# Three routing groups of 5, 5 and 6 batches instead of four of 4, and two elementwise steps of the experts exchanged between VectorE and GpSimd

## The reference

```python
h = layernorm(x) * (1 + ca) + sa
# attention: every token goes to 2 of 8 experts, by softmax of h @ gate
# per batch and expert: the last 256 of its tokens, in order of the sequence
q, k, v = q_w h, k_w[e] h, v_w[e] h          # q and k then squared into features
S = 0                                        # linear attention, chunk by chunk
out = (q k^T * causal) v + q S ; S = S + k^T v
x = x + ga * (rms_per_head(sum_2(weight * out)) @ o_w)
h = layernorm(x) * (1 + cb) + sb
h = swiglu(h @ lin0)
# experts: 8 routed ones, 4 chosen per token, and 2 shared ones
routed = sum_e combine[t, e] * ((silu(h w1_e) * (h w3_e)) @ w2_e)
h = swiglu((routed + shared) @ lin1)
x = x + gb * h
```

## Time and profile before

| | us |
|---|---|
| median of 3 runs | 1236.74 (1235.38 to 1238.14) |
| the profiled execution | 1226.49 |
| its span, first to last instruction | 1224.7 |
| busy: TensorE, VectorE, ScalarE, GpSimd | 1073.1, 913.7, 674.7, 489.9 |

### The profile page before, as it was taken

The page is one execution under the profiler, slowest core; times in us unless marked ns, Lnnn a source line. Parts: engine busy times, 40 slices in busy tenths (PEclk is TensorE's granted clock), DMA queues, the critical chain, the costliest instruction groups (busy, mean ns, idle before and its releaser), DMA issues. The chain is left out here.

```text
span 1224.7 us, 26738 instructions
## 1 busy us (share of the span) xinstructions
PE 1073.1 (88%) x9288; PEld 778.6 (64%) x9288; DVE 913.7 (75%) x2058; ACT 674.7 (55%) x1645; POOL 489.9 (40%) x450
## 2 busy tenths in 40 slices
PE   4865779999999877889999995988998899899997
PEld 3653546667777655667666664765666577677774
DVE  4785568788877666668778784888888987786774
ACT  2452245455555545656667552666666566555564
POOL 2046213312332444431221114656676644455552
PEclk9987679999999999999999997999999999899999
DMA  9972133323333333322222215321332322225230
GB/s 304 367 303 91 35 93 99 110 87 101 102 111 95 98 95 96 88 77 71 70 67 66 66 35 155 89 63 52 111 97 71 90 80 84 72 86 149 78 86 18
DMA packets 83586, 125.76 MB, mean 103 GB/s; under 512 B 9088, under 2 KB 65920, under 8 KB 79360
## 3 DMA queue, kind: packets, MB, share of 16 engines
q1 hardware_dynamic: 73216, 98.86, 26.5%
q0 software_dynamic: 10240, 25.18, 6.4%
HBM read 71.32 MB, written 52.69 MB: 101 GB/s over the span
## 5 line engine op out<-in xcount | busy, mean ns | idle before, releaser
L1489 DVE SCALAR_TENSOR_TENSOR att<-reach,endrel,wide 128x1024 f32<-128x1024 f32 x160 | 204.8, 1280 | 85.8 <-PE wide L1401 76.8
L1607 POOL TENSOR_TENSOR kvw<-kvw,hq 128x512 f32<-128x512 f32 x128 | 170.6, 1333 | 183.2 <-ACT kvw L1698 177.2
L900 POOL DMA_INDIRECT gst<-attended_rows,idxs x128 | 138.6, 1083 | 237.1 <-DVE att L1489 155.0
L252 POOL DMA_INDIRECT routed_rows<-hq,idxs x128 | 130.7, 1021 | 223.5 <-DVE att L1489 152.8
L1732 DVE TENSOR_TENSOR epp<-kvw,epp 128x512 fp32r<-128x512 f32 x160 | 138.2, 863 | 80.4 <-ACT epp L1706 77.8
L1654 PE MATMUL bank<-epp,w2p 128*128 128x512 f32 x480 | 166.3, 456 | 11.0 <-DVE epp L1732 10.9
L1644 PE MATMUL bank<-hp,w1p 128*128 128x512 f32 x480 | 142.0, 405 | 8.3 <-POOL hp L1560 6.2
L1376 PE MATMUL bank<-kvw,turned 128*128 x320 | 142.0, 526 | 5.1 <-ACT turned L1285 1.6
L1706 ACT ACTIVATE epp<-kvw 128x512 fp32r<-128x512 f32 x160 | 100.5, 628 | 79.1 <-DVE kvw L1739 74.4
L1644 PE MATMUL wide<-hp,w3p 128*128 128x512 f32 x480 | 141.4, 404 | 0.0
L1698 ACT ACTIVATE kvw<-bank 128x512 f32<-128x512 f32 x160 | 94.8, 593 | 79.8 <-PE wide L1644 79.3
(11 more groups left out here) (265 smaller groups left out, 1895.7 us busy)
## 6 DMA issues: line engine op xcount, KB each, us to landing
hq<-weight_rows SPq DMA_DIRECT2D x16, 2048.0 KB
routed_rows<-zero SPq DMA_DIRECT2D x4, 5120.0 KB, 24.6
rows<-routed_rows SPq DMA_DIRECT2D x80, 256.0 KB
attended_rows<-ob SPq DMA_DIRECT2D x80, 128.0 KB
out<-fin SPq DMA_DIRECT2D x16, 256.0 KB, 2.3
routed_rows<-hq,idxs POOLq DMA_INDIRECT x128
gst<-attended_rows,idxs POOLq DMA_INDIRECT x128
hq<-in_ew SPq DMA_DIRECT2D x3, 512.0 KB, 6.6
```

Source lines behind the costliest of these rows:

```text
L252: pool.indirect_dma_start(hs[s], bass.IndirectOffsetOnAxis(idxs[:, t, k:k + 1], 0), hq[:, t, :], None, bounds_check=BLOCKS[s] * P - 1, oob ...
L900: pool.indirect_dma_start(gst[:, u, k, :], None, orow[s], bass.IndirectOffsetOnAxis(idxs[:, t, k % TOPA:k % TOPA + 1], 0), bounds_check=BL ...
L1489: dve.scalar_tensor_tensor(out=att[:, n % 2, :, :], in0=reach[:, :, :].rearrange("p a c -> p (a c)").unsqueeze(1) .to_broadcast([P, 4, 2 * ...
L1607: pool.tensor_tensor(g, g, rows_of(b % 2, n, n + 1), ALU.mult).then_inc(s_eu, 1)
```

## The change

There are three parts.

**Groups and blocks.** `SUPER` is (5, 5, 6). The formula gives 48, 48 and 56 blocks, 152 in all, eight fewer. The tables of a group are made by functions that take one group, not several at once, and the comparison of block slots with segment ends, which was in two halves of 640 elements, is in three pieces of 640 (groups 0 and 1) and four of 672 (group 2). In stage one the first count comes one batch later (`COUNT = 8`), and the scatters of group 0 are 40 and wait from the tenth batch's q on. In stage two the scatters are 40 in iterations 0 to 32 and 48 in 34 to 74.

**Jobs.** `J1[b] = C0[1] + 30 + 10 * b` = 78 + 10b, eight iterations sooner. As the blocks are eight fewer too, a job stands at the same distance from the end of stage two as before.

**Experts.** VectorE multiplies the gate with the token's weight, right before its product with the up bank. GpSimd makes the low part of the unit before, for all ten experts.

```diff
-SUPER = (4, 4, 4, 4)
+SUPER = (5, 5, 6)
...
-        HALF = BLOCKS[0] // 2
...
+        CHUNKS = (3, 3, 4)
+        ROWS = tuple(n // c for n, c in zip(BLOCKS, CHUNKS))
...
-        CHOOSE1 = {4: 0, 9: 1, 13: 2, 16: 3}
-        CHOOSE2 = {5: 0, 10: 1, 14: 2}
-        EXPONENT = {6: 0, 11: 1, 15: 2}
-        COUNT = 7
-        TABLE = {1: 4, 2: 18, 3: 32}
-        WEIGHTS = 46
+        CHOOSE1 = {5: 0, 10: 1, 16: 2}
+        CHOOSE2 = {6: 0, 11: 1}
+        EXPONENT = {7: 0, 12: 1}
+        COUNT = 8
+        BASES = {1: -6, 2: 3}
+        SEGMENTS = {1: 0, 2: 7}
+        TABLE = {1: 11, 2: 26}
+        WEIGHTS = {1: 46, 2: 50}
...
                 for t in range(NT * SUPER[0]):
                     if t % 3 == 0:
-                        pool.wait_ge(s_qb, 9 + t // 3)
+                        pool.wait_ge(s_qb, 10 + t // 3)
                     for k in range(TOPA):
                         scatter(pool, t, k)
...
-        J1 = [C0[1] + 46 + PERIOD * b for b in range(NB)]
+        J1 = [C0[1] + 30 + PERIOD * b for b in range(NB)]
...
-                        begin, end = max(C0[s - 1] - 6, 0), C0[s] - 14
+                        begin = max(C0[s - 1] - 14, 0)
+                        end = begin + (32, 40)[s - 1]
                         while lo <= sent[0] < hi and (sent[0] - lo) * (end - begin) <= (n - begin) * (hi - lo):
                             if sent[0] == lo:
+                                pool.wait_ge(s_routed, s + 1)
                                 pool.wait_ge(s_z[s], 16)
                             scatter(pool, sent[0] // TOPA, sent[0] % TOPA)
                             sent[0] += 1
...
-                for k in range(UNITS):
+                for k in range(UNITS + 1):
                     b, n = divmod(k, NU)
-                    if n < E:
-                        if n == 0:
-                            pool.wait_ge(s_cb[b % 2], 16 * (b // 2 + 1))
-                        pool.wait_ge(s_es, k + 1)
-                        g = eg[:, k % RING, :].rearrange("p (i t) -> p i t", t=P)
-                        pool.tensor_tensor(g, g, rows_of(b % 2, n, n + 1), ALU.mult).then_inc(s_eu, 1)
+                    if k:
+                        pool.wait_ge(s_eh, k)
+                        pool.tensor_tensor(epp[:, (k - 1) % RING, 1, :], ep[:, (k - 1) % RING, :],
+                                           epp[:, (k - 1) % RING, 0, :], ALU.subtract).then_inc(s_el, 1)
                     post_pool(pool, NBK + k)
...
-                    if 1 <= k <= UNITS:
-                        dve.wait_ge(s_eh, k)
-                        dve.tensor_tensor(epp[:, (k - 1) % RING, 1, :], ep[:, (k - 1) % RING, :],
-                                          epp[:, (k - 1) % RING, 0, :], ALU.subtract).then_inc(s_el, 1)
                     if b < NB:
+                        dve.wait_ge(s_es, k + 1)
+                        if n == 0:
+                            dve.wait_ge(s_cb[b % 2], 16 * (b // 2 + 1))
                         if n < E:
+                            g = eg[:, k % RING, :].rearrange("p (i t) -> p i t", t=P)
+                            dve.tensor_tensor(g, g, rows_of(b % 2, n, n + 1), ALU.mult).then_inc(s_eu, 1)
                             dve.wait_ge(s_eu, E * b + n + 1)
-                        else:
-                            dve.wait_ge(s_es, k + 1)
+                        if k >= RING:
+                            dve.wait_ge(s_el, k - RING + 1)
                         dve.tensor_tensor(ep[:, k % RING, :], up_bank[k % RING][:, :], eg[:, k % RING, :],
                                           ALU.mult).then_inc(s_ep, 1)
```

More of the change, by code:

```diff
@@ L308, in bases, with keep_counts @@
[L308 to L315 removed]
+        def keep_counts(dve, s, ps):
+            one, two, upto, t, prod, pos, m, kept, row = views(s)
+            size = NT * SUPER[s]
+            chained(dve, dve.tensor_copy(pos, ps[:, 0:size * E].rearrange("p (t e) -> p t e", e=E)))
+            chained(dve, dve.tensor_copy(upto, ps[:, size * E:2 * size * E].rearrange("p (t e) -> p t e", e=E)))
@@ L316, in bases @@
+        def bases(dve, s, part):
+            one, two, upto, t, prod, pos, m, kept, row = views(s)
+            size = NT * SUPER[s]
+            cn = spare[:, 0:E * size].rearrange("p (e t) -> p e t", e=E)
+            sf = spare[:, 0:E * E].rearrange("p (e f) -> p e f", e=E)
+            nk, ba = nblk[:, s, :], base[:, s, :]
             if part == 0:
-                chained(dve, dve.tensor_tensor(cn, us[:, :, size - 1, :].unsqueeze(3).to_broadcast([P, many, E, size]),
-                                               steps128[:, :].unsqueeze(1).unsqueeze(1)
-                                               .to_broadcast([P, many, E, size]), ALU.is_gt))
+                chained(dve, dve.tensor_tensor(cn, upto[:, size - 1, :].unsqueeze(2).to_broadcast([P, E, size]),
+                                               steps128[:, 0:size].unsqueeze(1).to_broadcast([P, E, size]), ALU.is_gt))
@@ L325, in bases @@
                 chained(dve, dve.tensor_scalar(ba, ba, float(P), None, ALU.mult))
-                chained(dve, dve.tensor_tensor(ps, ps, ba.unsqueeze(2).to_broadcast([P, many, size, E]), ALU.add))
-        def indices(dve, s0, s1, s):
-            one, two, upto, t, prod, pos, m, kept, row = views(s0, s1)
-            chained(dve, dve.tensor_tensor(prod, (one, two)[s], pos, ALU.mult))
+                chained(dve, dve.tensor_tensor(pos, pos, ba.unsqueeze(1).to_broadcast([P, size, E]), ALU.add))
@@ new lines, in segments @@
+        def segments(dve, s, part):
+            one, two, upto, t, prod, pos, m, kept, row = views(s)
+            nb = SUPER[s]
+            se, sg, lm = (v[:, B0[s]:B0[s + 1], :] for v in (segend, segbeg, limit))
+            if part == 0:
+                chained(dve, dve.tensor_tensor(se, upto.rearrange("p (b i) e -> p b i e", i=NT)[:, :, NT - 1, :],
+                                               base[:, s, :].unsqueeze(1).to_broadcast([P, nb, E]), ALU.add))
+                chained(dve, dve.tensor_copy(sg[:, 0, :], base[:, s, :]))
+                chained(dve, dve.tensor_copy(sg[:, 1:nb, :], se[:, 0:nb - 1, :]))
+            else:
@@ L396, in table, with slot_weights @@
                 dve.sem_inc(s_tab, 1)
-        def slot_weights(dve, s0, s1, part):
-            one, two, upto, t, prod, pos, m, kept, row = views(s0, s1)
+        def slot_weights(dve, s, part):
+            one, two, upto, t, prod, pos, m, kept, row = views(s)
             if part == 0:
@@ L676, in _ @@
                 pe.transpose(bank[3][:, P:2 * P], mat[:, 3, :], ident[:, :]).then_inc(s_lt, 1)
-                for s in (1, 2):
-                    count(s, wide[:, s, :])
+                count(1, wide[:, 1, :])
                 pe.wait_ge(s_lc, 1)
@@ L757, in choose_first @@
                 def choose_first(s):
-                    one, two, left, t, prod, pos, m, kept, row = views(s, s + 1)
+                    one, two, left, t, prod, pos, m, kept, row = views(s)
                     dve.wait_ge(s_lg, B0[s + 1])
@@ L829, in _ @@
                 dve.wait_ge(s_cnt, NS)
-                keep_counts(dve, 1, NS, wide[:, 1:NS, :])
+                for s in range(1, NS):
+                    keep_counts(dve, s, wide[:, s, :])
         ph.close()
```

150 lines of the change are left out of this document (62 added, 88 removed).

## The result

The changed kernel takes 1224.17 us (median of 13 runs, 1220.7 to 1232.18), the kernel before in the same job 1232.32 (13 runs, 1227.27 to 1238.14). The ratio is 0.9933, with a 95% interval of 0.9913 to 0.9953: 8 us faster, where 43 were forecast. The forecast started from 1236.74, the median of three runs; that of all thirteen is 4.4 us lower. The profiled execution of the changed kernel took 1227.21 us (span 1225.5).

What follows compares the result with a forecast made beforehand. Limits: TensorE in the last stretch; in earlier experts a VectorE-ScalarE ring plus jobs; in attention, scatters and gathers cost extra. Terms +4 - 27 - 21 + 0.5, say -43, took 1236.74 to 1194 us; range 1174 to 1224.

Steps and rivals of the forecast that it cites:

- Part one: Attention: eight blocks without jobs go, at 3.10 us each, 24.8 us saved.
- Parts two and three: Attention: fewer scatters among gathers save 10 us (0 to 15); scatters packed closer lose 8 (0 to 12).
- Part four: Routing: 40 scatters for 32, starting one batch later, mostly hidden; 4 us lost, bounds -2 and +12.
- the 150 that the forecast had set: Routing: the scatters of stage one would be over before 150 us if the forecast was right.
- the forecast's bound of 12: Routing: upper bound of the loss, if the eight added scatters, 11.5 us, come onto the path.
- Part five: Experts with jobs: VectorE weights the gate, GpSimd makes the low part; 21 us saved, bounds 30 and nothing.
- so the two hardly meet: Experts: GpSimd's low part starts 0.63 us after the weighting, after ScalarE's high part, so their lock would seldom matter.
- queued behind the new waits: Experts: VectorE's product and job instructions, and GpSimd's gathers, stand behind the new waits; no separate size given.
- The last stretch: Experts from 1077 us on: TensorE has no gap, nothing gained; slower low part at the very end, +0.5 us.
- its sign of being wrong: End of the experts: batches above 23.5 us would show the forecast wrong; 23.2 would show it right.
- The rival of the lock: Experts: VectorE's weighting meets GpSimd's low part in every unit; slower, 1283 us, or 1248 at half; chance 0.06.
- The rival of GpSimd: Experts: GpSimd becomes the limit, a batch needs 31 us, the exchange gives 0; 1214 us, chance 0.17.

Runs made afterwards that it cites:

- x10: Changed kernel with silu kept in PSUM, gather ahead of the low part, last group's scatters over 48 blocks; 0.9729 on the starred chip (kernel before 1173.03 us).
- x5: Kernel before with the experts' exchange and silu written back into its PSUM bank; 0.9953 on the starred chip (kernel before 1173.03 us).
- x2: Changed kernel with the experts as before, so only the new groups and the jobs eight slots sooner; 0.981 of the kernel before.
- x3: Changed kernel with GpSimd's gather issued ahead of the low part in each unit of the experts; 0.9827 of the kernel before.
- x4: Changed kernel with silu written back into its PSUM bank, so the weighting reads one operand there; 0.979 of the kernel before.
- x6: Changed kernel with both silu kept in PSUM and the gather ahead of the low part; 0.971 of the kernel before.
- x13: Repeat of x2, the changed kernel with the experts as before; 0.9823 of the kernel before.
- x11: x2 with the jobs four slots sooner; 1.0011 on the starred chip (kernel before 1173.03 us).
- x12: Repeat of x10 on a chip without the star; 0.9639 of the kernel before, 1186.6 us against 1233.33.
- x7: x2 with the jobs four slots later; 0.9988 of the kernel before.

## Why the prediction was wrong

**Part one, eight blocks fewer (-24.8), right.** The changed kernel has 152 masks. On the chip with the star, where no block shows the delay, the masks of x10 go from 165.8 to 666.9 us and those of x5 from 154.8 to 680.2: 24.3 us less with eight blocks fewer. The whole attention is 552.9 - 524.5 = 28.4 us shorter; 3.3 of the other 4 lie between the last mask and the first product of the experts (10.6 us in x5, 7.3 in x10; before and after on the other chips 10.0 and 7.3), which no term had.

**Parts two and three (-10 and +8), right in the sum, too small in the price of packing.** Attention: 595.5, 605.4 and 602.9 before (mean 601.3), 571.6 to 580.9 on the new groups with the same scatters (mean of the changed kernel, x2, x3, x4, x6 and x13: 575.7), so -25.6 against -27. But the blocks 30 to 60 went from 93.3 us (blocks 30 to 60 of the kernel before, 269.0 to 362.3) to 106.4 in x13: 13 us, where the term had 8 for all. The mechanism that was named, a scatter behind another indirect DMA, is the one seen; the prediction priced it by mean spacing and didn't ask which scatters would stand back to back.

**Part four, the routing (+4), right in the mean on all chips but one; its steps were not.** The 40 scatters of the changed kernel, first and last:

```profile
98.00 1.21 POOL L253 DMA_INDIRECT routed_rows<-hq,idxs  x1 [11.36 <-ACT hq L561]
...
154.31 0.97 POOL L253 DMA_INDIRECT routed_rows<-hq,idxs  x1 [0.30 <-issue]
```

They take 57.3 us, as forecast (57.8), but begin at 98, not 91, and end at 155.3, past the 150 that the forecast had set. In the earlier trace rows 21 us lie between the last scatter's end and the first load of rows, which is now at 162.68: 7.4 us. The stage scatters by 7 us between executions: 153.9 to 161.5 with the old groups (mean of three 158.7), 157.8 to 165.3 with the new (mean of ten 162.0), so +3.3, not clear of that scatter. On the chip with the star it is 11.8 (x10) and 14.6 us (x11) more than in x5, as much as the forecast's bound of 12: there the rows are loaded 3.6 us behind the end of the last scatter, in x5 9.3.

**Part five, the exchange (-21), failed.** The step that fails is "so the two hardly meet". It compared the start of the weighting with the low part of the same unit. The low part of unit k - 1 and the weighting of unit k are what meets, as soon as VectorE is late by a job's instructions or GpSimd by a gather: 1018 ns for 73 weightings, and 687 with one operand in PSUM (x4). The price of an undisturbed one was right (0.70 forecast, 0.69 at 888.94, 0.687 in x4). The second thing it missed is ahead of that: "queued behind the new waits ... on GpSimd the gathers" was written down and given no price; it is 11 us by x3. Over the whole run VectorE's two or three instructions per unit went from 138.2 + 109.0 to 123.1 + 110.0 us, 14 less in 16 batches and not 3 in each. The exchange cost 11 to 12 us in the experts (484.8 against 473.8; 487.3 against 475.3), and with both causes gone it gains 15, so even then the 21 was a third too much.

**The last stretch (+0.5), twice that, and its sign of being wrong was met.** From batch 10 on a batch takes 23.1 us in both kernels, but from batch 9 to 10 it is 25.3 where it was 23.7, so batches 9 to 14 take (1196.33 - 1078.47) / 5 = 23.57 us, where 23.24 stood and 23.5 was the limit. From batch 9 to the end it is +1.1 us. With the PSUM operand (x4, x6, x12) the step from 9 to 10 is 23.6. The rows answer to the earlier trace rows:

```profile
1143.03 1.29 POOL L1598 TENSOR_TENSOR epp<-kvw,epp 128x512 fp32r<-128x512 f32 x1 [0.88 <-ACT epp L1698]
...
1143.74 0.86 PE L1646 MATMUL bank<-epp,w2p 128*128 128x512 f32 x3
...
1144.57 0.69 DVE L1728 TENSOR_TENSOR kvw<-kvw,hq 128x512 f32<-128x512 f32 x1 [1.41 <-ACT kvw L1690]
```

Here the low part is over at 1144.32 and the weighting starts at 1144.57: they keep apart, with 0.25 us to spare. Not everywhere in this stretch: three of the eight weightings of the next batch meet GpSimd (0.98, 0.86 and 1.55 us at 1150.87, 1155.93 and 1160.98), and TensorE, which has no gap there, doesn't feel it.

**The sum:** +3.3 - 25.6 + 11 to 12 gives -10 to -11 by the stages, and the timed ratio -8. The time is just above the range (1224.17 against 1224). The rival of the lock had the cause and the stretch (0.3 us a unit for those with jobs, where an added 0.32 was measured for a weighting), but had every unit meet, and hung its sign on the last stretch, where three of eight do and cost nothing. The rival of GpSimd had the gathers and their part as 0; it is below 0.

## What to carry to other kernels

Before two elementwise streams change places between VectorE and GpSimd, lay the instruction of each beside the one of the neighbouring unit and not only of its own, with the engine late by a job; where they can meet, give VectorE's one operand in PSUM. Where work with a long latency (a gather) shares a queue with something that waits, put it ahead of the wait and look at who stands behind its reader. Before a job is moved by a few slots, look at what must have landed by the border of the next group of batches. A whole change that comes out near zero may be two halves of opposite signs: take it apart first.

## What was not expected of the hardware

Two chips differ by 5% on the same kernel, 1173 against 1232 to 1236 us, in the attention and the routing and hardly in the experts (461.0 against 459.0 us with the same code): on the one a block between scatters takes 3.0 to 3.1 us however they stand (three kernels, all in one job), on the others ScalarE stands idle up to 3.8 us and VectorE 2.2 where three scatters follow each other, and the granted clock of these blocks falls to 0.95. A gain that rests on the spacing of indirect DMAs is worth 1% on the one kind and nothing on the other.

An instruction of 36 elements a row on VectorE (L1053, 0.19 us when undisturbed) took 3.0 to 3.3 us four times of 18 in x7, when GpSimd had two instructions one behind the other beside it. Four slots of shift in the jobs, either way, cost 2%, the later ones in greater part because the weights of every fourth batch come late.
